# A sigmoid recurrence moved from two 32-column product tiles to four of 16, its programs written out without semaphore clears

## The reference

```python
Wx = jnp.einsum('bti,hi->bth', x, W)
flat = Wx.reshape(B * T, H)
mean, var = jnp.mean(flat, axis=0), jnp.var(flat, axis=0)
Wx = ((flat - mean) * jax.lax.rsqrt(var + BN_EPS) * gamma + beta).reshape(B, T, H)
Vt = V.T
def step(yt, wx_t):
    yt = jax.nn.sigmoid(wx_t + yt @ Vt)
    return (yt, yt)
_, ys = jax.lax.scan(step, jnp.zeros((B, H)), jnp.swapaxes(Wx, 0, 1))
```

## Time and profile before

| | us |
|---|---|
| median of 3 runs | 4314.11 |
| lowest and highest | 4312.28, 4323.86 |
| span of the profiled execution | 4315.0 |
| the recurrence in it, first to last sigmoid | 2478.4 to 4310.1 |
| PE, ACT, VectorE, GpSimd busy over the span | 4170.7, 2016.0, 1330.3, 119.6 |

### The profile page before, as it was taken

One profiled execution on the slowest core, in us unless ns is written; L12 is line 12 of the kernel. 1 busy time (PEld: TensorE's weight loads), 2 busy tenths in 40 slices (PEclk: granted clock), 3 DMA queues, 4 the chain that ended last, 5 costly groups with the idle time before them and its releaser, 6 DMA issues.

```text
span 4315.0 us, 139757 instructions
## 1 busy us (share of the span) xinstructions
PE 4170.7 (97%) x57266; PEld 3076.9 (71%) x57266; DVE 1330.3 (31%) x2528; ACT 2016.0 (47%) x8972; POOL 119.6 (3%) x243
## 2 busy tenths in 40 slices
PE   7999999999989999999999899999999999999999
PEld 2799999995342699999995266666666666666665
DVE  3555533334555655533334700000000000000000
ACT  5002334334554102243344366666666666666666
POOL 1000000000000000000000000000000000000000
PEclk8899999999999999999999899999999999999999
DMA  5000000002447200000005400000000000000000
GB/s 138 17 0 0 0 0 0 0 0 74 133 113 216 61 0 0 0 0 0 0 0 143 124 15 21 15 21 21 15 21 21 15 21 21 15 21 21 15 21 18
DMA packets 178401, 144.32 MB, mean 33 GB/s; under 512 B 110910, under 2 KB 177502, under 8 KB 178014
## 3 DMA queue, kind: packets, MB, share of 16 engines
q1 hardware_dynamic: 178014, 138.21, 12.1%
HBM read 79.19 MB, written 58.98 MB: 32 GB/s over the span
## 4 chain that ended last, share of the span: by engine, by line
PE 93%; DVE 3%; issue 2%; ACT 2%; SPq 1%; DMA 0%; ACTq 0%; DVEq 0%; PEldq 0%
PE ps L930 22%; PE ps L767 21%; PE ps L745 18%; PE ps L835 16%; PE ps L830 3%; PE ps L571 3%; PE ps L563 1%; PE ps L582 1%; PE ps L592 1%; PE ps L718 1%; PE ps L606 1%; DVE rstd L1162 1%; PE ps L808 1%; PE ps L636 1%; PE ps L685 1%
## 5 line engine op out<-in xcount | busy, mean ns | idle before, releaser
L930 PEld LDWEIGHTS ps<-xl,vt 65*32 65x32 f32 x28800 | 1036.0, 108 | 717.0 <-ACT xl L1145 686.2
L1145 ACT ACTIVATE xl<-ps 64x8 f32<-64x8 f32 x7200 | 1176.5, 170 | 656.8 <-PE ps L930 652.8
L930 PE MATMUL ps<-xl,vt 65*32 65x8 f32 x28800 | 1422.6, 183 | 20.6
L835 PE MATMUL ps<-idle 128*32 128x256 bf16 (+1 forms) x5894 | 1374.9, 273 | 0.0
L767 PE MATMUL ps<-xl,taps 128*128 128x128 f32 (+2 forms) x7880 | 921.3, 280 | 4.7 <-DVE xl L1334 4.7
L767 PEld LDWEIGHTS ps<-xl,taps 128*128 128x128 f32 x7880 | 920.8, 191 | 5.6 <-issue 5.3
L745 PE MATMUL ps<-split 128*128 128x400 f32 x4140 | 781.0, 352 | 12.8 <-DVE split L1329 12.8
L745 PEld LDWEIGHTS ps<-split 128*128 128x128 f32 x4140 | 779.0, 190 | 16.5 <-issue 15.2
L1418 DVE TENSOR_TENSOR xl<-xl 64x320 f32<-64x320 f32 x180 | 125.1, 695 | 1709.1 <-PEq L934 1699.7
L1003 ACT ACTIVATE img<-xl 128x144 f32 x788 | 365.8, 464 | 556.5 <-DVE xl L1311 556.5
L835 PEld LDWEIGHTS ps<-idle 128*32 128x32 bf16 x5894 | 584.5, 99 | 22.1 <-issue 10.2
(11 more groups left out here) (153 smaller groups left out, 1685.0 us busy)
## 6 DMA issues: line engine op xcount, KB each, us to landing
ring<-in_x_dram SPq DMA_DIRECT2D x144, 200.0 KB, 3.7
x_dram<-sums SPq DMA_DIRECT2D x144, 200.0 KB, 3.2
t_dram<-sums SPq DMA_DIRECT2D x72, 200.0 KB, 3.6
ring<-t_dram SPq DMA_DIRECT2D x72, 200.0 KB, 3.9
ring<-x_dram SPq DMA_DIRECT2D x72, 200.0 KB, 3.7
xl<-x_dram SPq DMA_DIRECT2D x45, 320.0 KB, 4.6
out_dram<-xl SPq DMA_DIRECT2D x45, 320.0 KB, 3.5
img<-in_L_ffn_weight_dram SPq DMA_DIRECT2D x4, 512.0 KB
```

The lines of the kernel that those rows point to most:

```text
L835: pe.matmul(PS[bank][0:32, 0:n], idle[:, 0:32], idle[:, 0:n], start=True, stop=True)
L930: last = pe.matmul(PS[2 * s + h][c * 32:(c + 1) * 32, t * HB:(t + 1) * HB], vt[:, c * 32:(c + 1) * 32], prev, start=False, stop=True, skip ...
L1145: act.activation(yb[0:64, s % 2, h * HB:(h + 1) * HB, t], PS[s % 2 * 2 + h][0:64, t * HB:(t + 1) * HB], ACT.Sigmoid).then_inc(step_y[h][s ...
```

## The change

- The 64 channels of `yb`, `x2b` and `ob` now stand in four quadrants of 16: channel 16 q + c is on partition 32 q + c (`quad`, `QC` = 16, `QROWS` = 112). `vt` has its rows in the same places and zeros between them.
- A product is four tiles of 16 output columns (`QUADS` = 4), over 112 rows, into four quadrants of the bank. The sigmoid works on 112 partitions. `fill_input` also has four tiles and takes its weights from `ident`.
- Batch scale and bias are applied by GpSimd in `stage_segment` (one multiply-add with `bnm[:, 6:7]` and `bnm[:, 8:9]`); `wsc`, the bias row, PE's transpose of the bias and the copy on VectorE go. The first segments are staged when the statistics are there.
- `step_mm` and `step_y` are one counter for each half, never cleared; waits use the running count. `seg_done` goes; VectorE waits for both `step_y`.
- The programs of ACT, VectorE and GpSimd are written out in full. SyncE keeps its loop, with four DMAs for the load and four for the store.
- The filler is 128 columns after half 0's product; after half 1's it is 384, or 128 behind a part of `fill_input`, which now follows half 1. Four matmuls on zeros write the four banks once at the start.

```diff
@@ -108,6 +111,9 @@
         def half(buf, h):
             return buf[h * 64:(h + 1) * 64]
 
+        def quad(buf, q):
+            return buf[32 * q:32 * q + QC]
+
 
         TAPS_HOME = (xl, sums)
         wraw = [home[:, 0:2 * C * KT] for home in TAPS_HOME]
...
         hidden_t = xl[:, 2048:4096]
         mixed_out = xl[:, 4096:4608]
         outt = xl[0:64, 4608:5120]
-        yb = xl[0:65, 0:2 * SEG * B].rearrange("p (s t b) -> p s b t", s=2, b=B)
-        x2b = xl[0:64, 1920:1920 + BODY * SEG * B].rearrange("p (b t) -> p b t", b=B)
-        ob = xl[0:64, 3840:3840 + BODY * SEG * B].rearrange("p (b t) -> p b t", b=B)
-        wsc = [xl[:, 5760 + h * 64:5824 + h * 64] for h in range(2)]
+        yb = xl[0:QROWS, 0:2 * SEG * B].rearrange("p (s t b) -> p s b t", s=2, b=B)
+        x2b = xl[0:QROWS, 1920:1920 + BODY * SEG * B].rearrange("p (b t) -> p b t", b=B)
+        ob = xl[0:QROWS, 3840:3840 + BODY * SEG * B].rearrange("p (b t) -> p b t", b=B)
         stage = [xl[:, 5952 + j * SEG * HB:5952 + (j + 1) * SEG * HB].rearrange("p (t b) -> p t b", b=HB) for j in range(2)]
         swap = [xl[0:64, LEFT + h * HB * WP:LEFT + (h + 1) * HB * WP].rearrange("p (b j) -> p b j", b=HB) for h in range(2)]
...
@@ -199,8 +204,8 @@
         bn_std, rnn_c = sem("bn_std"), sem("rnn_c")
         pool_done, taps_blank = sem("pool_done"), sem("taps_blank")
         passed = sem("passed")
-        step_mm, step_y = ([[sem(f"{n}{h}_{j}") for j in range(2)] for h in range(2)] for n in ("step_mm", "step_y"))
-        seg_done, x2_in, added, out_st = (sem(n) for n in ("seg_done", "x2_in", "added", "out_st"))
+        step_mm, step_y = ([sem(f"{n}{h}") for h in range(2)] for n in ("step_mm", "step_y"))
+        x2_in, added, out_st = (sem(n) for n in ("x2_in", "added", "out_st"))
         staged, filled = sem("staged"), sem("filled")
 
 
...
@@ -449,11 +455,13 @@
             sp_norm(sp, 3)
             sp.wait_ge(rnn_ready, 1)
             with sp.Fori(0, NIT) as i:
-                sp.dma_start(x2b, nat_all(x2_dram)[:, :, ds(i * (BODY * SEG), BODY * SEG)]).then_inc(x2_in, 16)
+                now = ds(i * (BODY * SEG), BODY * SEG)
+                for q in range(QUADS):
+                    sp.dma_start(quad(x2b, q), nat_all(x2_dram)[q * QC:(q + 1) * QC, :, now]).then_inc(x2_in, 16)
                 sp.wait_ge(added, i * BODY + (BODY + 2))
-                sp.dma_start(nat_all(out.rearrange("b c h w -> b c (h w)"))[:, :, ds(i * (BODY * SEG), BODY * SEG)],
-                             ob).then_inc(out_st, 16)
-            sp.wait_ge(out_st, 16 * (NIT + 1))
+                for q in range(QUADS):
+                    sp.dma_start(nat_all(out.rearrange("b c h w -> b c (h w)"))[q * QC:(q + 1) * QC, :, now], quad(ob, q)).then_inc(out_st, 16)
+            sp.wait_ge(out_st, 16 * QUADS * NIT)
 
 
         def place_taps(eng, l):
...
@@ -468,9 +476,12 @@
                         last = eng.tensor_copy(dst[:, d0 + 2:d1 + 3, op, :], wt[l][q // 2][:, k0:k0 + 2 * (d1 - d0) + 1:2, q % 2, :])
             last.then_inc(taps_ready[l], 1)
 
-        def stage_segment(pool, j, z, t):
+        def stage_segment(pool, seg):
+
+            z, t = seg // SLOT_SEGS % 2, seg % SLOT_SEGS * SEG
             own(pool)
-            pool.tensor_copy(stage[j].rearrange("p t b -> p b t"), slots[:, z, 0:HB, ds(t, SEG)]).then_inc(staged, 1)
+            pool.tensor_scalar(stage[seg % 2].rearrange("p t b -> p b t"), slots[:, z, 0:HB, t:t + SEG], bnm[:, 6:7], bnm[:, 8:9],
+                               ALU.mult, ALU.add).then_inc(staged, 1)
 
         @block.gpsimd
         def _(pool):
...
@@ -515,24 +526,15 @@
             pool.memset(taps[:, :], 0.0).then_inc(taps_blank, 1)
             pool.wait_ge(taps_blank, 1)
             place_taps(pool, 1)
-            pool.wait_ge(ln[3].normed, NG * N2)
-            for j in range(2):
-                stage_segment(pool, j, 0, j * SEG)
-            pool.wait_ge(staged, 2)
-            alone(pool.memset(yb[64:65], 1.0))
+            pool.wait_ge(rnn_ready, 1)
+            for seg in range(2):
+                stage_segment(pool, seg)
             for h in range(2):
-                alone(pool.memset(yb[0:64, 1, h * HB:(h + 1) * HB, SEG - 1], 0.0))
-                pool.sem_inc(step_y[h][1], SEG)
-            with pool.Fori(0, SLOT_SEGS // 2 - 1) as q:
-                for j in range(2):
-                    pool.wait_ge(filled, q * 2 + (j + 1))
-                    stage_segment(pool, j, 0, q * (2 * SEG) + (j + 2) * SEG)
-            with pool.Fori(0, SLOT_SEGS // 2) as q:
-                for j in range(2):
-                    pool.wait_ge(filled, q * 2 + (SLOT_SEGS - 1 + j))
-                    stage_segment(pool, j, 1, q * (2 * SEG) + j * SEG)
-            pool.wait_ge(filled, 2 * SLOT_SEGS - 1)
-            stage_segment(pool, 0, 0, 0)
+                alone(pool.memset(yb[:, 1, h * HB:(h + 1) * HB, SEG - 1], 0.0))
+                pool.sem_inc(step_y[h], 1)
+            for seg in range(2, SEGS + 1):
+                pool.wait_ge(filled, seg - 1)
+                stage_segment(pool, seg)
 
         TAP_BANKS = (((4, 5, 6), (4, 5, 6)), ((2, 3, 4), (5, 6, 7)))
 
...
@@ -825,9 +827,9 @@
         def fill_input(pe, j, part):
 
             h, t0 = part // FILLS, part % FILLS * FILL_T
-            acc = PS[2 * j + h][0:64, 0:SEG * HB].rearrange("p (t b) -> p t b", b=HB)
-            for c in range(2):
-                last = pe.matmul(acc[c * 32:(c + 1) * 32, t0:t0 + FILL_T, :], wsc[1 - h][:, c * 32:(c + 1) * 32],
+            for q in range(QUADS):
+                acc = quad(PS[2 * j + h], q)[:, 0:SEG * HB].rearrange("p (t b) -> p t b", b=HB)
+                last = pe.matmul(acc[:, t0:t0 + FILL_T, :], ident[:, (1 - h) * 64 + q * QC:(1 - h) * 64 + (q + 1) * QC],
                                  stage[j][:, t0:t0 + FILL_T, :], start=(t0 == 0), stop=True, skip_group_check=True)
             return last
 
...
@@ -909,42 +912,36 @@
             pe.matmul(PS[7][:, 0:1], fold[:, :], bnm[:, 0:1], start=True, stop=True).then_inc(bn_pe, 1)
             pe.wait_ge(bn_dve, 2)
             pe.matmul(PS[7][:, 2:3], fold[:, :], bnm[:, 3:4], start=True, stop=True).then_inc(bn_pe, 1)
-            pe.wait_ge(bn_dve, 3)
-            pe.transpose(PS[7][0:1, 128:192], bnm[0:64, 8:9], ident[0:64, 0:64]).then_inc(bn_pe, 1)
-            pe.wait_ge(rnn_ready, 1)
-
-
-
+            for bank in range(4):
+                pe.matmul(PS[bank][:, 0:SEG * HB], idle[:, 0:128], idle[:, 0:SEG * HB], start=True, stop=True)
             pe.wait_ge(staged, 1)
             for part in range(2 * FILLS):
                 last = fill_input(pe, 0, part)
             last.then_inc(filled, 1)
-            for i in range(NIT * BODY // 2):
-                for s in range(2):
-                    for t in range(SEG):
-                        for h in range(2):
-                            pe.wait_ge(step_y[h][s] if t else step_y[h][1 - s], t if t else SEG)
-                            images = slice(h * HB, (h + 1) * HB)
-                            prev = yb[:, s, images, t - 1] if t else yb[:, 1 - s, images, SEG - 1]
-                            for c in range(2):
-                                last = pe.matmul(PS[2 * s + h][c * 32:(c + 1) * 32, t * HB:(t + 1) * HB], vt[:, c * 32:(c + 1) * 32],
-                                                 prev, start=False, stop=True, skip_group_check=True)
-                            last.then_inc(step_mm[h][s], 1)
-                            if t == 0:
-                                pe.sem_clear(step_y[h][1 - s])
-                                if h == 1:
-                                    pe.sem_inc(seg_done, 1)
-                            if h == 0 and t < 2 * FILLS:
-                                if t == 0:
-                                    pe.wait_ge(staged, i * 2 + (s + 2))
-                                last = fill_input(pe, 1 - s, t)
-                                if t == 2 * FILLS - 1:
-                                    last.then_inc(filled, 1)
-                            else:
-                                keep_clock(pe, 256, 4)
-            for h in range(2):
-                pe.wait_ge(step_y[h][1], SEG)
-            pe.sem_inc(seg_done, 1)
+            def step(s, t, h, done):
+                pe.wait_ge(step_y[h], done + 1)
+                images = slice(h * HB, (h + 1) * HB)
+                prev = yb[:, s, images, t - 1] if t else yb[:, 1 - s, images, SEG - 1]
+                for q in range(QUADS):
+                    last = pe.matmul(quad(PS[2 * s + h], q)[:, t * HB:(t + 1) * HB], vt[0:QROWS, q * QC:(q + 1) * QC], prev,
+                                     start=False, stop=True, skip_group_check=True)
+                last.then_inc(step_mm[h], 1)
+
+            for seg in range(SEGS):
+                s = seg % 2
+                for t in range(SEG):
+                    step(s, t, 0, seg * SEG + t)
+                    keep_clock(pe, 128, 4)
```

(52 more changed lines are left out.)

15 lines of the change are left out of this document (9 added, 6 removed).

## The result

The changed kernel takes 4711.0 us (4706.5 to 4721.3) where the kernel before takes 4316.1 beside it: ratio 1.092 [1.090, 1.093]. It is slower, as forecast, but by 395 us and not by 73, and lies far above the range of 4305 to 4462. The profiled execution took 4721.3 us and has a span of 4719.6.

The account below looks back on a forecast made before the run. Bound by chained product and sigmoid latencies in the recurrence: 4315.0 + 75.6 (3600 steps x 21 ns) - 4.0 (loop turns) + 1.9 (tail), less 0.9 against the median, gave 4387.6 us; range 4305 to 4462.

Parts of the forecast that it names:

- What bounds the kernel: Sigmoid recurrence: product and sigmoid latencies chained, neither engine full; one nanosecond more on a half's loop costs 3.6 us.
- Issue side: Product's loads and matmuls: two more tiles cost 14 ns, 16 fewer columns save 13; net +1 ns a step.
- Finishing side: Last matmul's end to sigmoid: about 10 ns for each further column tile, two more tiles, +20 ns a step.
- Sigmoid: ACT's sigmoid in the recurrence: reading 112 partitions where it read 64 costs nothing, 0.
- Fillers, contraction, VectorE, GpSimd: Recurrence: new filler columns, 112 rows not 65, and changed VectorE and GpSimd work; each 0, the engines' within 1 us.
- Loops: Segment boundaries: ACT's loop turn at every fourth goes, 0.09 x 44 = -4.0 us; the 0.06 at each boundary stays.
- Tail: After the last sigmoid: three further SyncE issues of 0.625 us for the stores add up to 1.9 us.
- PE is starved or slowed: Rival, chance 0.10: PE's 36 to 52 records a step outrun its instruction packets, or the clock drops, over 4560 us.
- The prediction's own sign of being wrong: Profile after: the finish does not grow, or PE shows idle time that no sigmoid ended.
- the rival's other half, the clock: Recurrence products at clock 0.50 span 0.28 not 0.23 us: 180 us, over 4560; chance 0.10 shared with starvation.

Follow-up runs that it names:

- e9: e2 with the eight loads of a product widened from 16 to 32 columns, four tiles kept; 4464.5 us, 1.034.
- e14: e10 with input filling in the product's two tiles of 48 columns and fillers 64 columns wide; 4428.3 us, 1.027.
- e13: e11 with product, input filling and filler all 64 columns wide; 5250.7 us, 1.216.
- e2: Changed kernel with the old programs (cleared counters, ACT and VectorE in loops) and PE's recurrence in a loop; 4391.3 us, 1.018.
- e6: Kernel before, fillers cut into 6 pieces in filling steps and 5 in others, 36 PE records a step; 4427.8 us, 1.026.
- e4: Kernel before, fillers cut into 8 pieces and 6, 40 PE records a step; 4623.4 us, 1.072.
- e11: e7 with each product in one tile of 64 columns; 7026.0 us, 1.627.
- e10: e2 with each product in two tiles of 48 columns; 6633.1 us, 1.536.
- e12: e8 with its fillers back at 128 rows; 6262.8 us, 1.450.
- e8: e7 with products and fillers of 64 rows, no bias row, GpSimd adding the bias; 4864.2 us, 1.126.
- e3: Kernel before with all programs of the recurrence written out and counters never cleared; 4309.9 us, 0.999.
- e7: e3 with ACT's two waits ahead of a segment's first sigmoid exchanged; 4308.3 us, 0.997.

## Why the prediction missed

The forecast was 4387.6 and the result 4711.0. Step by step, in the prediction's order:

- **What bounds the kernel** was read rightly for the kernel before: two chained latencies, and a nanosecond a step is 3.6 us. It was taken over unasked for the kernel after, which has a second bound, the supply of PE's instructions.
- **Issue side, +1 ns:** measured 0 (61 and 61). Both halves of the step hold: e9 prices the 16 columns at 13 to 14 ns, which the four further loads give back.
- **Finishing side, +20 ns:** measured +20 (47 to 67), and e14 and e13 confirm its form.
- **Sigmoid, 0:** measured +7 (170 to 177). The step took one long sweep with two shapes as proof that partitions cost nothing; 25 us.
- **Not in the sum:** the last matmul's record is 6 or 7 ns shorter with 16 columns. The two misses cancel; the period is 525 where the sum gives 526.
- **Fillers, contraction, VectorE, GpSimd:** 0, and e2 agrees. GpSimd takes 627 ns where its copy took 469, hidden as said.
- **Loops, -4.0:** in the changed kernel all boundaries are 584 against 525, +59, and nothing further at the fourth. Unrounded, the turn was 639 against 565 ns in the kernel before, so the term should have been 0.074 x 44 = 3.3. e2, which keeps ACT's loop, should be 4387.6 + 4.0 = 4391.6 and is 4391.3. That it agrees to 0.3 us is luck: the misses on sigmoid and last record cancel, and e2 has a loop on PE besides.
- **Tail, +1.9:** the window after the last sigmoid is 5.6 us and was 4.7: +0.9.
- **The step that failed** is the rival "PE is starved or slowed". It named the packets and the rise of records to 36 to 52, and set it aside with 132 matmuls and 128 loads in 2.00 us, "but that run was short". It was 260 instructions, hardly more than one packet, so it showed how fast PE runs what it already holds, not how fast more comes. The only long stretch in the trace was the earlier trace rows, 22.7 ns an instruction; the forecast needed 12.4 for 1.9 ms. No row reached that far, so the chance of 0.10 was too low and the range had no right to leave the case out. The prediction's own sign of being wrong, PE idle time that no sigmoid ended, is what the page shows. The step also priced only the rival's other half, the clock. The trace has low clock too: from 2799.99 to 2801.30 the granted clock is 0.50 and the products of one half start at 2799.99, 2800.53 and 2801.07, 0.54 apart. Low clock costs 0.015 a step here and not 0.05 as taken from the earlier trace rows: the changed product spans 0.24 there and 0.23 at full clock. (In e6, with its cut fillers, a step at half clock took 0.61 for 0.505, above.) The lost time is the supply's. The window:

```profile
2799.99:2801.30 1.31, 1.31 (x70) 0.97 (x61) 0.00 (x0) 0.89 (x5) 0.00 (x0) 0.50 0.04 13
```

The size follows: 3600 steps x 42.4 records x 14.6 ns = 2229 us, against 3600 x 0.525 + 180 x 0.06 = 1901 by latency. The larger of the two holds, and the difference, 328 us, is the miss of 323. The 14.6 is the changed kernel's own; with the 14.9 of e4, whose tiles are the old ones, it would be 2274 us, 2% more. What sets the price of a packet stays open.

## What to carry to other kernels

Where an engine's program is written out, count its instructions over the time they have, and compare that with the longest stretch of written-out code in the trace, not with a burst; packets of the instruction queue times 256 say what is fetched, and idle time ended by "issue" every 256 records says that the limit is reached. If it is, put the engine in a loop whose body stays resident (one turn of e2 has 1696 PE records and fetches nothing), or merge instructions: each tile split is paid in instructions as well as in the finish of 10 ns a tile. Keep all matmuls that should overlap at tile heights and widths that have been seen to overlap.

## What the runs showed of the hardware that was not expected

- Written-out code on PE came at 67 to 68 records a us in the mean and not faster (e6, e4, the changed kernel), one packet of 256 in 3.75 us or a little more; in stretches at full clock it was 69 to 71. The same stream in a loop ran at 80.
- Products and fillers of some tile sizes don't overlap: 64 or 48 columns against 32 (e11, e10), 64 rows against 128 (e12). At the same granted clock of 0.50 that cost 1775 us (e11 over e13) and 1399 us (e12 over e8). Columns of 16 against 32 (the changed kernel) and 48 against 64 (e14) overlap, and so do 65 or 112 rows against 128.
- A sigmoid over 8 columns takes 170 ns on 64 partitions and 177 on 112.
- With fillers of half the rows (e8), or with all tiles 64 columns wide in one-tile products (e13), the clock was granted at 0.50 throughout the recurrence, though PE is shown as busy all the time. The cause stays open.
- A wait that has long been met costs the sigmoid 0.06 us if it stands ahead of the wait that is met late (e3), and nothing behind it (e7).
